# A second buffer for rows that are only looked at, and one place less for q, k and v

## What is computed

```
x = x + attn(layernorm(x)):
  q, k, v = h @ wq.T + bq, h @ wk.T + bk, h @ wv.T + bv      # each [tokens, 32 heads, 32]
  scores  = einsum('bshd,bstd->bsht', q, k) / sqrt(32)       # 32 x 32 for each token
  context = einsum('bsht,bstd->bshd', softmax(scores), v)
x = x + ffn(layernorm(x)):
  w -> table[nearest(w / absmax(block of 64))] * absmax      # for w1, w2, w3
  out = (silu(h @ w1.T) * (h @ w2.T)) @ w3.T
```

## Time and profile before

| | |
|---|---|
| profiled execution | 2107.1 us, span 2105.3 us, mean granted TensorE clock 0.961 |
| median of 3 executions | 2105.9 us |
| attention in full swing, 144 to 600 us | PE busy 428.91 us of 456, DVE 385.27, ACT 143.36, clock 0.99 |
| handover, 600 to 640 us | PE busy 36.31 us of 40, DVE 26.55, clock 0.74 |
| handover, 640 to 725 us | PE busy 50.97 us of 85, DVE 71.02, ACT 48.25, clock 0.62 |
| feed-forward, from 760 us | PE busy 1335.24 us of 1345, clock 1.00 |
| looks (L600) | 66, 1.2 us each |
| load into ff_raw | 66 of 512 KB or less, median 3.7 us from issue to landing |

### The profile page before, as it was taken

One profiled execution on the slowest core, in us unless ns is written; L12 is line 12 of the kernel. 1 busy time (PEld: TensorE's weight loads), 2 busy tenths in 40 slices (PEclk: granted clock), 3 DMA queues, 4 the chain that ended last, 5 costly groups with the idle time before them and its releaser, 6 DMA issues.

```text
span 2105.3 us, 30875 instructions
## 1 busy us (share of the span) xinstructions
PE 1975.9 (94%) x10272; PEld 1073.6 (51%) x10272; DVE 1839.8 (87%) x1846; ACT 1495.2 (71%) x1665; POOL 1164.6 (55%) x674
## 2 busy tenths in 40 slices
PE   4699999999988499999999999999999999999999
PEld 3376767676776344444444444444444444444442
DVE  8578888888877899899999989999899999999972
ACT  5524232332324698998989999899998989998872
POOL 0100101001012558779788787877879787786964
PEclk8799999999986599999999999999999999999999
DMA  7123334343322662222212121212122212212214
GB/s 290 44 87 119 129 103 139 120 139 110 119 87 99 197 204 46 55 49 50 52 48 54 45 59 40 60 40 60 42 58 44 55 45 55 58 42 56 36 36 160
DMA packets 219616, 175.24 MB, mean 83 GB/s; under 512 B 143664, under 2 KB 186672, under 8 KB 219568
## 3 DMA queue, kind: packets, MB, share of 16 engines
q1 hardware_dynamic: 217456, 166.23, 28.1%
q10 hardware_dynamic: 2112, 8.39, 1.0%
HBM read 115.34 MB, written 25.17 MB: 67 GB/s over the span
## 4 chain that ended last, share of the span: by engine, by line
PE 60%; DVE 2%; ACT 2%; issue 1%; POOL 0%; ACTq 0%; DMA 0%; POOLq 0%; SPq 0%; DVEq 0%
PE bank L1404 13%; PE bank L1406 13%; PE bank L1405 13%; PE bank L1425 7%; PE bank L1426 7%; PE bank L1427 7%; DVE bank L1274 2%; ACT signs L1173 2%; DVE w_nat L1274 0%; DVE bank L1268 0%; ACTq L1253 0%; DMA w3T_lo<-half 0%; ACT half L1181 0%; DVE hidden L1282 0%; POOL w_nat L1085 0%
## 5 line engine op out<-in xcount | busy, mean ns | idle before, releaser
L1274 DVE SCALAR_TENSOR_TENSOR bank<-signs,bank 128x1024 f32<-128x1024 int8 (+2 forms) x792 | 964.5, 1218 | 53.4 <-ACT signs L1173 26.3
L1173 ACT ACTIVATE signs<-w_nat,compare_bias 128x1024 int8<-128x1024 f32 (+2 forms) x924 | 987.0, 1131 | 0.8 <-DVE w_nat L1274 0.6
L1404 PE MATMUL bank<-x2T_hi,w12T_hi 128*128 128x512 f16 x1376 | 524.5, 381 | 10.8 <-DMA w12T_lo<-half 4.7
L1405 PE MATMUL bank<-x2T_lo,w12T_hi 128*128 128x512 f16 x1376 | 524.1, 381 | 0.0
L1406 PE MATMUL bank<-x2T_hi,w12T_lo 128*128 128x512 f16 x1376 | 524.0, 381 | 0.0
L772 PE MATMUL bank<-wT_hi,xT_hi 128*128 128x512 f16 x768 | 299.7, 390 | 12.3 <-issue 12.3
L772 PE MATMUL bank<-wT_hi,xT_lo 128*128 128x512 f16 x768 | 299.2, 390 | 0.0
L727 ACT ACTIVATE probs<-probs 128x1024 f32<-128x1024 f32 x16 | 16.9, 1059 | 377.1 <-DVE probs L653 377.1
L1425 PE MATMUL bank<-w3T_hi,hT_hi 128*128 128x512 f16 x704 | 268.2, 381 | 4.8 <-DVE hidden L1282 4.1
L1426 PE MATMUL bank<-w3T_lo,hT_hi 128*128 128x512 f16 x704 | 267.3, 380 | 0.0
L1427 PE MATMUL bank<-w3T_hi,hT_lo 128*128 128x512 f16 x704 | 267.2, 380 | 0.0
(11 more groups left out here) (96 smaller groups left out, 2667.9 us busy)
## 6 DMA issues: line engine op xcount, KB each, us to landing
ff_raw<-in_L_ffn_w SPq DMA_DIRECT2D x63, 512.0 KB, 3.7
w_nat<-in_L_ffn_w SPq DMA_DIRECT2D x63, 512.0 KB, 3.9
x_nat<-in_L_attn_hidden_states SPq DMA_DIRECT2D x16, 512.0 KB, 3.8
x_res<-in_L_attn_hidden_states SPq DMA_DIRECT2D x16, 512.0 KB, 4.5
x<-x_res SPq DMA_DIRECT2D x16, 512.0 KB, 2.6
acc<-x ACTq DMA_DIRECT2D x4, 2048.0 KB, 14.9
out<-acc SPq DMA_DIRECT2D x16, 512.0 KB, 2.6
w_raw<-in_L_attn_wq SPq DMA_DIRECT2D x8, 512.0 KB, 6.7
```

The costliest lines, as they stand in the source:

```text
L1173: nc.scalar.activation(signs[0:rows, ring(v, k), 0:cols], w_nat[0:rows, v % SLOTS, 0:cols], ACT.Sign, scale=COMPARE[SUMMED[k]][0], bias=co ...
L1274: V.scalar_tensor_tensor(to, part, HALF_STEP[SUMMED[k]], total, ALU.mult, ALU.add).then_inc(sign_used, 1)
L1404: nc.tensor.matmul(dst, hi, x2T_hi[:, toks, c], start=c == 0, stop=False)
L1405: nc.tensor.matmul(dst, hi, x2T_lo[:, toks, c], start=False, stop=False)
```

## The change

ff_raw gets two places, each with its own semaphore, and qkv loses one, so that the two keep their common size. v is evacuated into the place of q (`m % 2`); its first half waits for q's transpose of the same row (`q_ready`), and q's first half for v's transpose of the row before (`v_ready`). Looks alternate between the places: in the loop the place of the q-th of nine looks of a turn is q % 2, so the ninth and the next turn's first use the same one. A load waits for the look two before it, except the first of a loop's turn, which waits for the look just before it (`behind` is 2). The order of issues on SyncE and of instructions on VectorE stays.

```diff
-        qkv = sb("qkv", [P, 3, E])
+        qkv = sb("qkv", [P, 2, E])
...
-        ff_raw = sb("ff_raw", [P, E])
+        ff_raw = sb("ff_raw", [P, 2, E])
...
-        ff_in = sem("ff_in")
+        ff_in = [sem("ff_in0"), sem("ff_in1")]
...
-                return [(it * 3 + 2 + q // 3, q % 3, it * 9 + 6 + q, P) for q in places]
-            tiles = {0: (0,), 1: (1,), T - 2: (FT - 1, FT)}.get(n, ())
-            return [(tile, m, tile * 3 + m, P if tile < FT else REST) for tile in tiles for m in range(3)]
+                return [(it * 3 + 2 + q // 3, q % 3, it * 9 + 6 + q, P, q % 2, it * (5, 4)[q % 2] + 3 + q // 2 + 1, 1 + (q == 0))
+                        for q in places]
+            if n < 2:
+                return [(j // 3, j % 3, j, P, j % 2, j // 2 + 1, 1) for j in range(3 * n, 3 * n + 3)]
+            first = 6 + 9 * LOOP
+            return [(j // 3, j % 3, j, P if j < 3 * FT else REST, (j + 1 - first) % 2, (5, 4)[(j + 1 - first) % 2] * LOOP + 3 + (j - first) // 2 + 1, 1)
+                    for j in range(first, first + 6)] if n == T - 2 else []
...
-            def load_ff(tile, m, j, rows):
+            def load_ff(tile, m, j, rows, slot, times, behind):
                 first = tile * P
-                sp.wait_ge(absmax_done, j + 1)
+                sp.wait_ge(absmax_done, j + behind)
...
-                    sp.dma_start(ff_raw[0:rows], (w1, w2)[m][bass.ds(first, rows), :]).then_inc(ff_in, 16)
+                    sp.dma_start(ff_raw[0:rows, slot], (w1, w2)[m][bass.ds(first, rows), :]).then_inc(ff_in[slot], 16)
...
-            def evacuate(n, u, m, h):
+            def evacuate(n, u, it, m, h):
                 i = 2 * m + h
                 cols = slice(h * BANK, (h + 1) * BANK)
+                if m == 2 and h == 0:
+                    dve.wait_ge(q_ready, n + 1)
+                if m == 0 and h == 0 and not (it is None and n == 0):
+                    dve.wait_ge(v_ready, n)
                 dve.wait_ge(projected, 6 * n + i + 1)
-                nc.vector.scalar_tensor_tensor(qkv[:, m, cols], bank[:, (6 * u + i) % PROJ_RING], un_scale[:, m:m + 1],
+                nc.vector.scalar_tensor_tensor(qkv[:, m % 2, cols], bank[:, (6 * u + i) % PROJ_RING], un_scale[:, m:m + 1],
...
-            def look_at(tile, m, j, rows):
+            def look_at(tile, m, j, rows, slot, times, behind):
 
-                dve.wait_ge(ff_in, 16 * (j + 1))
+                dve.wait_ge(ff_in[slot], 16 * times)
...
-                                        qkv[:, 2].rearrange("p (h d) -> p d h", d=HD)).then_inc(v_ready, 1)
+                                        qkv[:, 0].rearrange("p (h d) -> p d h", d=HD)).then_inc(v_ready, 1)
...
-            dve.sem_inc(absmax_done, 1)
+            dve.sem_inc(absmax_done, 2)
```

More of the change, by code:

```diff
@@ L513, in load_ff @@
                 if m < 2:
-                    sp.dma_start(ff_raw[0:rows], (w1, w2)[m][bass.ds(first, rows), :]).then_inc(ff_in, 16)
+                    sp.dma_start(ff_raw[0:rows, slot], (w1, w2)[m][bass.ds(first, rows), :]).then_inc(ff_in[slot], 16)
                 else:
-                    sp.dma_start(ff_raw[:, 0:C * rows].rearrange("p (t h) -> p t h", t=C),
-                                 w3.rearrange("(t p) h -> p t h", p=P)[:, :, bass.ds(first, rows)]).then_inc(ff_in, 16)
+                    sp.dma_start(ff_raw[:, slot, 0:C * rows].rearrange("p (t h) -> p t h", t=C),
+                                 w3.rearrange("(t p) h -> p t h", p=P)[:, :, bass.ds(first, rows)]).then_inc(ff_in[slot], 16)
             def step(n, u, it, project=True, normalize=True, attend=True, end=True, feed=None):
@@ L599, in look_at @@
                     to = absmax[part, tile, m, 0:NB] if m < 2 else absmax[:, tile, m, 0::P // rows]
-                nc.vector.tensor_reduce(to, ff_raw[part, 0:blocks * BLOCK].rearrange("p (b e) -> p b e", e=BLOCK),
+                nc.vector.tensor_reduce(to, ff_raw[part, slot, 0:blocks * BLOCK].rearrange("p (b e) -> p b e", e=BLOCK),
                                         AX.X, ALU.max, apply_absolute_value=True).then_inc(absmax_done, 1)
@@ L618, in step @@
                 if attend:
-                    evacuate(n - 1, 1 - u, 2, 1)
+                    evacuate(n - 1, 1 - u, it, 2, 1)
                 if normalize:
@@ L638, in step @@
                     if project:
-                        dve.wait_ge(absmax_done, 3 * FT + 3 + 1)
+                        dve.wait_ge(absmax_done, 3 * FT + 3 + 2)
                     next(feed)
                 if project:
-                    evacuate(n, u, 0, 0)
+                    evacuate(n, u, it, 0, 0)
                 look()
                 if project:
-                    evacuate(n, u, 0, 1)
+                    evacuate(n, u, it, 0, 1)
                 if feed and project:
@@ L685, in step @@
                 if project:
-                    evacuate(n, u, 1, 0)
+                    evacuate(n, u, it, 1, 0)
                 look()
                 if project:
-                    evacuate(n, u, 1, 1)
+                    evacuate(n, u, it, 1, 1)
                     dve.wait_ge(evacuated, 6 * n + 4)
@@ L696, in step @@
                 if project:
-                    evacuate(n, u, 2, 0)
+                    evacuate(n, u, it, 2, 0)
                 look()
@@ L891, in feed_forward @@
         acc = sb("acc", [P, T, E])
-        spare = g["ff_raw"]
+        spare = g["ff_raw"][:, 0]
         squares = spare[:, 0:(FT + 1) * 2 * NB].rearrange("p (t m b) -> p t m b", m=2, b=NB)
```

## The result

The changed kernel takes 2091.6 us (median of 4 executions, 2090.1 to 2093.3) against 2105.2 us before on the same chips: a ratio of 0.9933, 95% interval 0.9921 to 0.9944, so 14 us or 0.7% faster. It lies in the forecast range and on the forecast side, but 12 us above the forecast value of 2080, on the 2091 of rival C and just under the range's upper end of 2092. The profiled execution took 2091.9 us with a span of 2090.0.

A forecast was written before the change was run, and what follows sets the result against it. The prediction took the ring of TensorE and VectorE in the attention, before about 720 us, as the bound. Saving 23.3 us there and 2.5 at the handover, 25.8 in sum, gave 2080 us, range 2070 to 2092.

The forecast's parts named there:

- rival C: VectorE's first ff_raw wait stays as before, its load wedged between store and next load: pair 70.17 us, 2091; chance 0.18.
- A: The forecast itself for the whole kernel, held likeliest: 2080 us; chance 0.52.
- the first waits: VectorE's wait for ff_raw between the evacuations of q's halves in each attention step; forecast 0.2 to 0.6 us each.
- the ring: Attention loop of TensorE and VectorE, each releasing the other's next work; a step costs 33.82 us plus the first wait.
- c: c(n): TensorE has finished the context products of attention step n; c to t by VectorE: 20.47 us plus the wait.
- t: t(n): TensorE starts the 8 transposes of x_res in attention step n; from t to c 13.35 us.
- step 1: VectorE's second ff_raw wait, between the evacuations of k's halves, up to 4.1 us, goes entirely.
- step 2: VectorE's first ff_raw wait: its load moves forward by 0.87 us, leaving 0.79 us a pair; bounds 0 and 2.53.
- step 3: A pair of attention steps takes 68.43 us instead of 72.17; with six pairs and 0.9, 23.3 us saved at t(14).
- steps 4 and 5: Attention to feed-forward: scores of step 15 at full clock, its context at half clock; 2.5 us kept of 10.4.
- Rival B: At the handover the clock doesn't fall before step 15's context, or is back soon: 33.7 us gained, 2072; chance 0.2.
- step 6: VectorE's two added waits on its own transposes cost 0; at 0.15 us each in 16 steps, 4.8 us at most.

The follow-up runs named there:

- e1: The changed kernel with the second look's load of a step issued ahead of SyncE's wait for x_res and the store of x_res: 2074.1 us.
- e2: The changed kernel with the third look's load of a step held until the second look is done: 2085.0 us.
- e3: The changed kernel with the second look's load issued between the wait for x_res and the store of x_res: 2081.5 us.
- e5: The changed kernel with 12 dense passes, results overwritten, on TensorE in step 15 where it stands 2.71 us for p_diag: 2082.5 us.
- e4: The kernel before with only v evacuated into q's place and both added waits, ff_raw keeping one buffer in use: 2106.5 us against 2106.2.
- e7: The changed kernel with 6 dense passes, results overwritten, on TensorE in step 15 ahead of the context: 2082.5 us, its profiled execution 2090.7.

## Why the prediction was right in kind and off in size

The time lies inside the range because the range was drawn to take in rival C. The case held likeliest, A, did not happen, and the first waits, 1.04 to 1.45 us, show the sign that the prediction names for C, waits above 1 us.

- The bound, the ring from c over L624 and xT_lo to t: right. Its terms measured 13.64 for 13.65 and 20.15 for 20.17. e1 to e3 confirm that the first wait counts about one to one: 15.4, 9.9, 7.0 and 0 us of waits go with 2091.6, 2085.0, 2081.5 and 2074.1 us, and with t(14) at 585.35, 579.57, 576.26 and 568.71.
- The second wait (step 1 of the working): right, gone, and VectorE's new spare time is spent waiting for c.
- The first wait (step 2): this is the step that failed, as a size. It put r, the first wait, at 0.79 us a pair; it is about 2.4, 15.4/13 = 1.18 a step. The issue moved forward even more than put, by 1.08 us for 0.87, but the time from issue to look was kept at the 3.8 us of a load with the store 1.5 us in front and the next load 5 us behind, and in the closer group it is 4.7. The row that was to speak for this, a load of x landing in 3.9 us behind the stores of x2, had a large load behind it too, but two smaller stores in front of it; it was not the nearest case. The bound of 2.53 a pair, drawn from the whole old wait, was the better value. That error is 1.6 us a pair, 9.6 us over the six pairs, most of the 12 us between forecast and time. Rival C described it, with a pair of 70.17 us for 70.03.
- The time at t(14) (step 3): 598.55 - 585.35 = 13.2 us gained, where 23.3 was the sum.
- The handover (steps 4 and 5): right. L624 of step 15 follows c(14) 0.2 us later, TensorE does not stand before the scores, and they run at full clock. p_diag ends 24.7 us after c(14) (25.3 forecast), TensorE stands 2.71 us (2.4 to 3), the clock falls and stays down through the narrow products. From t(14) to L624 of step 16 it is 642.97 - 585.35 = 57.62 us and was 59.60, with the row below from the trace before, so 2.0 us are kept (2.5 forecast) of some 10. e5 shows the rest: 9 us come back once the idle time is filled. Rival B did not happen here; in e3's trace, with the same idle time, it did. The prediction gave it 0.2, one execution of four in e1 and e3 and none in the changed kernel and e2 fit that, and what decides stays open. The lower bound in step 5 should read 1.9 and not 1.7 us (657.9 less 637.2 + 18.8), which moves nothing else.

```profile
658.15 1.23 DVE L616 TENSOR_TENSOR probs<-bank,inv_sum 128x1024 f32<-128x1024 f32 x1 [0.27 <-PE bank L799]
```

- The clock's return: the rule of the Trainium skill cited there (TensorE: Matmul & The Clock Gate, Part 1: The HAM clock gate) would, by the prediction's estimate, have had c(15) 6 us earlier. From 624 to 627 us TensorE was busy 3.00 of 3.00 us at 0.50, and the context lasted 19.4 us: the measurement stands against it.
- The own waits (step 6): 0, as taken (e4). t(2) came 0.4 us earlier, for the 0.9 of step 3.
- From 760 us on the two kernels are alike, TensorE busy 1320 us of 1330.

The best version, e6, issues the second look's load ahead of the wait for x_res and the store, and fills the 2.7 us: 2064.9 us, 41 us or 1.9% under the kernel before.

## What to carry to other kernels

A second buffer moves a load forward only as far as the next thing that stands before it in its queue, and it may then arrive among other large transfers: compute the landing from a load with the same neighbours, or issue it ahead of the unrelated wait. In a ring of two engines a wait counts by its place: 54 us of waits taken from VectorE were worth 14 us, while the 15 us that were left, in front of the one result that TensorE stands for, were worth 17. Here an idle time of 2.7 us on TensorE, before a stretch of narrow products, mostly cost 9 us, three times its own length, and 12 passes to nowhere were cheaper.

## What was not expected of the hardware

- A transfer is slowed by what is issued after it: the wait for the same load became 0.42 us shorter when the next load, 1.28 us behind it in step 8, was held back (e2). A store of 512 KB went from 2.6 us to landing in the kernel before to 4.9 to 5.4 between two loads (e3).
- The clock can fall after 1.41 us of idle time (e7) and stay after 2.70 (e3). In the trace before, idle times up to 1.82 us at t(n) had kept it and those from 1.94 had not; in e4 2.18 us kept it and 2.09 had not. The length of the idle time alone does not decide.
